# Self-attention and a Mamba block: the layer norm's Newton rounds move from GpSimd to VectorE, the root mean square's are spread over three steps

## What is computed

```python
# layer 0
energy = einsum('bnd,bdm->bnm', q, k); attn = softmax(energy, -1)
x = gamma * einsum('bcn,bmn->bcm', v, attn) + x
# layer 1, on tokens u of (4, 4096, 256)
mu = mean(u, -1); var = mean((u - mu) ** 2, -1)
u = (u - mu) * rsqrt(var + EPS) * norm_g + norm_b          # the layer norm
... in projection, causal conv of 4 taps, silu, scan over the tokens ...
y = y * silu(z)
y = y * rsqrt(mean(y * y, -1) + EPS) * rms_w               # the root mean square
out = y @ out_w.T
x = x + out_img * sigmoid(squeeze_excite(mean(out_img)))
```

## Time and profile before

| | |
|---|---|
| median of 3 runs | 3138.42 us (3137.31 to 3141.98) |
| the profiled execution, own time | 3134.2 us |
| its span | 3132.1 us |
| granted TensorE clock, mean | 0.982 |
| TensorE busy | 2969.5 us (95%) |
| TensorE weight loads busy | 2322.8 us (74%) |
| VectorE busy | 2038.2 us (65%) |
| GpSimd busy | 2006.3 us (64%) |
| ScalarE busy | 1922.7 us (61%) |

### The profile page before, as it was taken

How to read it: one execution, slowest core, us unless ns; L and a number is a source line. 1 busy time by engine, 2 the same in 40 slices (tenths; PEclk the granted TensorE clock), 3 DMA queues, 4 the chain that set the end, 5 groups by cost and what they waited for, 6 DMA issues and landing times. The chain is left out here.

```text
span 3132.1 us, 63156 instructions
## 1 busy us (share of the span) xinstructions
PE 2969.5 (95%) x21208; PEld 2322.8 (74%) x21208; DVE 2038.2 (65%) x3417; ACT 1922.7 (61%) x3742; POOL 2006.3 (64%) x3087
## 2 busy tenths in 40 slices
PE   6899999999999999999999999999999999999984
PEld 3767777777777777777777777777778777777763
DVE  5556666666766676676676666676666667676654
ACT  2555666666656666666665666666666666666652
POOL 2446666667756666666776656666676767777763
PEclk9999999999999999999999999999999999999996
DMA  4111111121321121222220122211221011111121
GB/s 123 49 44 33 45 58 54 35 61 40 100 71 65 58 84 48 89 77 70 83 95 30 57 85 65 78 66 64 73 90 36 30 63 62 56 63 50 55 95 67
DMA packets 101970, 200.99 MB, mean 64 GB/s; under 512 B 18480, under 2 KB 41392, under 8 KB 97264
## 3 DMA queue, kind: packets, MB, share of 16 engines
q1 hardware_dynamic: 98192, 195.08, 18.6%
q10 hardware_dynamic: 3456, 1.86, 0.2%
HBM read 131.21 MB, written 64.75 MB: 63 GB/s over the span
## 5 line engine op out<-in xcount | busy, mean ns | idle before, releaser
L723 POOL TENSOR_TENSOR p_lo<-p,p_hi 128x512 f16<-128x512 f32 x1024 | 1219.6, 1198 | 836.8 <-ACT p_hi L886 709.1
L879 ACT ACTIVATE p<-p_et 128x512 f32<-128x512 f32 x1024 | 612.2, 598 | 638.4 <-PE p_et L1138 591.7
L1156 PE MATMUL acc<-v_hi,p_hi 128*128 128x257 f16 x4096 | 955.3, 274 | 4.0 <-DVE work L1464 3.8
L1158 PE MATMUL acc<-v_lo,p_hi 128*128 128x256 f16 x4096 | 952.9, 273 | 0.0
L1420 DVE TENSOR_REDUCE maxes<-p_mx 128x1 f32<-128x1024 f32 x508 | 620.2, 1221 | 500.0 <-PE p_mx L1117 499.8
L886 ACT ACTIVATE p_hi<-p 128x512 f16<-128x512 f32 x1024 | 644.4, 629 | 10.0
L1164 PE MATMUL acc<-v_hi,p_lo 128*128 128x257 f16 x4096 | 623.0, 274 | 16.7 <-POOL p_lo L723 16.7
L1156 PEld LDWEIGHTS acc<-v_hi,p_hi 128*128 128x128 f16 x4096 | 399.8, 98 | 125.0 <-issue 54.6
L1158 PEld LDWEIGHTS acc<-v_lo,p_hi 128*128 128x128 f16 x4096 | 400.9, 98 | 118.6 <-issue 50.4
L1164 PEld LDWEIGHTS acc<-v_hi,p_lo 128*128 128x128 f16 x4096 | 400.0, 98 | 69.9 <-POOL p_lo L723 17.6
L1138 PE MATMUL p_et<-qs,kst 98*128 98x256 f16 x2048 | 393.2, 273 | 12.4 <-ACT p L879 11.7
(11 more groups left out here) (213 smaller groups left out, 4163.5 us busy)
## 6 DMA issues: line engine op xcount, KB each, us to landing
work<-rows_d SPq DMA_DIRECT2D x32, 1024.0 KB, 5.1
xin<-in_x_dram SPq DMA_DIRECT2D x48, 512.0 KB, 5.2
xr<-in_x_dram SPq DMA_DIRECT2D x32, 512.0 KB, 3.7
x_d<-x1c SPq DMA_DIRECT2D x31, 512.0 KB, 3.0
og_d<-og SPq DMA_DIRECT2D x29, 512.0 KB, 2.7
mix_x<-x_d SPq DMA_DIRECT2D x25, 512.0 KB, 4.7
mix_o<-og_d SPq DMA_DIRECT2D x24, 512.0 KB, 5.6
out_dram<-mix_o SPq DMA_DIRECT2D x24, 512.0 KB, 2.8
```

What stands on the lines that cost most here:

```text
L723: e.tensor_tensor(p_lo[:, n % RING, :], p32[:, n % P32S, :], p_hi[:, n % RING, :], ALU.subtract).then_inc(lo_pool, 1)
L879: e.activation(p32[:, n % P32S, :], p_et[:, :], ACT.Exp).then_inc(exp_done, 1)
L1156: e.matmul(acc[:, t, 0:C + 1], p_hi[:, r, at:at + P], v_hi[:, 2 * k + kk, 0:C + 1], start=(k == 0 and kk == 0), stop=False)
L1158: e.matmul(acc[:, t, 0:C], p_hi[:, r, at:at + P], v_lo[:, 2 * k + kk, :], start=False, stop=False, skip_group_check=True)
```

## The change

`norm` goes from GpSimd. VectorE runs the three rounds itself at step 3 (`K_LN + 2`), as ten instructions: a round is a TENSOR_TENSOR and two SCALAR_TENSOR_TENSORs, each with a drain ahead, and one more makes the product with the mean. The semaphore `ln_guess` between the two engines falls away. `root_mean` on GpSimd runs one round at each of the steps 23, 24 and 25 in place of three at step 23.

```diff
-            def newton(w):
-                for _ in range(3):
+            def newton(w, steps=3):
+                for _ in range(steps):
...
-            def norm(g):
-                e.wait_ge(ln_guess, g + 1)
-                e.tensor_scalar(nw[:, 2, :], mv[:, :, 0], -1.0, None, ALU.mult)
-                newton(nw)
-                e.tensor_tensor(nw[:, 4, :], nw[:, 2, :], nw[:, 3, :], ALU.mult).then_inc(ln_ready, 1)
-
-            def root_mean(g):
-                e.wait_ge(rms_guess, g + 1)
-                newton(rw).then_inc(rms_ready, 1)
+            def root_mean(g, part):
+                if part == 0:
+                    e.wait_ge(rms_guess, g + 1)
+                ins = newton(rw, 1)
+                if part == 2:
+                    ins.then_inc(rms_ready, 1)
...
-                if 0 <= s - 1 < G and K == K_LN + 2:
-                    norm(s - 1)
...
-                    if K == K_RMS + 1:
-                        root_mean(g)
+                    if K_RMS + 1 <= K < K_RMS + 4:
+                        root_mean(g, K - K_RMS - 1)
...
-                    rsqrt_guess(nw, nwi, mv[:, :, 1], 1.0, 1e-5).then_inc(ln_guess, 1)
+                    rsqrt_guess(nw, nwi, mv[:, :, 1], 1.0, 1e-5)
+                if K == K_LN + 2:
+                    for _ in range(3):
+                        e.drain()
+                        v.tensor_tensor(nw[:, 1, :], nw[:, 3, :], nw[:, 3, :], ALU.mult)
+                        e.drain()
+                        v.scalar_tensor_tensor(nw[:, 1, :], nw[:, 1, :], -0.5, nw[:, 0, :], ALU.mult, ALU.mult)
+                        e.drain()
+                        v.scalar_tensor_tensor(nw[:, 3, :], nw[:, 1, :], 1.5, nw[:, 3, :], ALU.add, ALU.mult)
+                    e.drain()
+                    v.scalar_tensor_tensor(nw[:, 4, :], mv[:, :, 0], -1.0, nw[:, 3, :], ALU.mult, ALU.mult)\
+                        .then_inc(ln_ready, 1)
```

More of the change, by code:

```diff
@@ L391, in conv_attention_mamba_kernel @@
         filled = sem("filled")
-        ln_guess = sem("ln_guess")
         ln_ready = sem("ln_ready")
```

## The result

The changed kernel took 3152.27 us (median of 6 runs, 3148.54 to 3154.12) beside 3137.86 us for the kernel before (6 runs), a ratio of 1.0044 [1.0031, 1.0057]: 14 us slower, over the 0.2% that this kernel's measurement can tell. The forecast was 3145 with a range of 3131 to 3157: the direction and the range held, but the forecast loss of 6.7 us was less than half of the 14.4 that came.

A forecast was written before the change was run, and what follows sets the result against it. TensorE was taken to bound the kernel, so only its waits count. -5.7 (`xw`) + 5.1 (qk) + 4.2 (se1) + 3.6 (mix) - 0.5 (slot 32) = +6.7 us, giving 3145 us; range 3131 to 3157.

The forecast's parts named there:

- Rounds: Step 3, VectorE: the ten instructions take 4.4 us, two or three of them 0.5 to 1.2 us beside GpSimd's.
- The first rival: Step 3: no collisions, the ten run in 2.45 us; -9.3 us in sum, 3129 us; chance 0.15.
- `xw`: Step 8: TensorE's waits for this GpSimd result nearly vanish; a gain of 5.7 us, of at most 15.1.
- The common slots: Slots 3, 5, 6, 7, 13, 15, 21, 23, 24, 25, 28, 29: gain at step 8, 12 x 0.37 = 4.4 us.
- "mr": TensorE's fill at step 8: still needs VectorE's `yt`, so it waits 0.4 us in nearly every slot.
- qk and se1: Step 4 fills wait for late `yt`: slots 4, 12, 20 lose 3 x 1.7 us, slots 10, 18, 26 3 x 1.4.
- the mix slots: Slots 14, 22, 30, with two `mix_o` instructions behind: 1.2 us lost each, 3.6 us; bounds 0.4 gain, 2.4 loss.
- the carried part alone: Slots 14, 22, 30: 1.7 us late minus 0.46 us idle, 1.2 us carried into steps 6 to 8.
- the second collision: Slots 14, 22, 30: `mix_o` beside GpSimd's `p_lo`, up to 1.2 us more, not in the sum.
- The third rival: Steps 5 and 6: scan and `max_parts` collide with GpSimd's moved work; 12 us more over 20 slots, 3157 us; chance 0.12.
- Root mean square: GpSimd, steps 23 to 25: last round comes later, but 3.3 us are left before ScalarE needs it; cost 0.

The follow-up runs named there:

- the PSUM version: Changed kernel with nine of the ten step 3 instructions taking one input from PSUM, and the guess's first two instructions using PSUM: 3120.46 us, 0.9949.
- the root mean square together: Changed kernel with all three Newton rounds of the root mean square back at step 23 of GpSimd: 3152.09 us, 1.0039.
- the version with the whole norm in PSUM: Against the PSUM version, the guess's third instruction and the norm's last one read PSUM too: 3121.77 us, 0.9947.

## Why the prediction was right, and where its size was wrong

- **Rounds: held.** Ten instructions in 4.73 us for 4.4; three of them wait for GpSimd's, each until the end of that very instruction. The first rival (no collisions) needed under 0.3 us of waits and got 2.1. That VectorE's waits for GpSimd are the cause, and that they hang on where the operands lie, is shown by the PSUM version, in which nine instructions of the same size at the same place take 0.16 to 0.17 us beside the same GpSimd while the tenth still waits. The Trainium skill's rule (SBUF — State Buffer, "SBUF: two separate sides": GpSimd and a VectorE instruction with two SBUF inputs hold a pair of ports exclusively, the other blocks for the whole instruction) agrees: 0.52 to 1.04 us with both inputs in SBUF beside GpSimd, at most 0.17 with one in PSUM. The same page of the Trainium skill counts in VectorE's two-port modes, which it lists for copy, cast and `tensor_scalar`. The guess, three TENSOR_SCALARs, agrees (0.47 to 0.64 us on average, and 0.16 to 0.17 with PSUM on one side), and I had left that half out.
- **`xw`: held.** The common slots gained 0.48 us for 0.37, since `yt` now ends 0.1 us sooner in the step; "mr" waits 0.36 us for 0.4.
- **qk and se1: the wait held, its price didn't always.** 1.44 us longer for 1.7, and 1.35 (1.14 in slot 26) for 1.4. Slots 12 and 10 cost just that, slot 20 1.2 us. Slot 4 cost 3.1 us and steps 4 to 6 of slot 18 3.0, with a clock of 0.90 and 0.86 behind the wait; 16.1 x 0.10 is 1.6 us and 12 x 0.14 is 1.7 us, which is what they lost beyond their waits. In the other run of nearly the same program (the root mean square together) slot 4 cost 1.45 us and slot 10 4.5: which of these slots it hits differs between the two executions.
- **The term that was too small: the mix slots.** "I take 1.2, the carried part alone: 3.6 us" measured 14.9. The bound of 2.4 us each was too low as well. I had named the second collision (`mix_o`, 1.2 us) and set it to nothing. It came (2.66 for 1.40 us), and made a third: `max_parts`, late by it, met three `p_lo` in a row. The waits are 4.02 us for 1.16 before, 2.9 us a slot. The other 2.3, 1.5 and 2.5 us go with a clock of 0.84 to 0.92 around a wait of 3.34 us, which no term of my sum had. The run with only those three slots on GpSimd took it all away.
- **The third rival (the reserve breaks in every slot): no.** "mr" waits 0.36 us in the common slots. It broke where other work of VectorE stood behind the rounds.
- **Luck in it.** The range held 3152 because its upper end, 3157, was that of this third rival, which did not come. With the mix slots at my own bound of 2.4 us each the sum would have been 3149. And slots 0, 1, 2, 9, 11, 17, 19 and 27, for which I had no term, gave 2.8 us back, 2.2 of them in slots 9 and 17 with their long waits for `p_lo`.
- **Root mean square: held.** Cost 0, by two runs.

The sum over the slots is +18.7 us, -1.1 behind them. Of it I put some 6 us in the mix slots and 3 in slots 4 and 18 down to the lower clock; that is argued from rows of the same stretches, not shown by a run of its own. In slot 21 TensorE waited 1.79 us for `vst_lo` at step 23 in place of 1.50, and the clock stood at 1.2 GHz for 3.4 us behind it, which together are what it lost there. In slot 29 it waited 0.99 us for ScalarE's `p` at step 16. What made these two waits longer is left open; neither is so in the run with the mix slots on GpSimd, where slot 25 has such a wait for `p` instead.

## What to carry to other kernels

Before work goes into an engine's idle time, look at what the neighbour that can hold it up does at that moment: here a 0.16 us instruction of VectorE took up to 1.17 us, as long as the `p_lo` of GpSimd that it met, and a chain of ten met up to three. Small VectorE chains escape by a few columns in an idle PSUM bank, as result or one input; here that turned 14 us of loss into 16 to 18 of gain, and it paid again for small instructions that had been there all along. Price a late transfer slot by slot, with the work that stands behind it, and keep room for the clock: in slot 4 a wait that grew by 1.44 us cost 3.1. And before a gain or loss of one slot is put down to a change, look whether it moves by itself: slots 10 and 26 differed by 1.5 and 1.6 us between executions by the clock at step 16 alone.

## What the runs showed of the hardware that I had not expected

- Instructions with one input and a result in SBUF waited for GpSimd like those with two inputs: TENSOR_SCALAR up to 0.60 us and CAST up to 1.05 us on 128x2, while a TENSOR_REDUCE from SBUF to SBUF on the same columns took 0.160 to 0.163 us in all 64, 35 of them begun beside a running GpSimd instruction. These are `mcol` and `mparts`, in the version with the whole norm in PSUM.
- TensorE's waits for GpSimd's `p_lo` did not grow in the versions whose VectorE instructions no longer wait: at step 3 of slots 1, 9 and 17 they stayed between 15.4 and 17.6 us in sum in all versions (16.7 before).
- Behind equal waits of TensorE (1.67 and 1.80 us) the granted clock was lower in some slots (0.86, 0.90) and not in others (1.00).
